# The first mixture's up and down products as separate lists in the order of a fused transformer kernel on one core

## What is computed

```python
# layer 1: two shared experts and eight routed ones, two of them per token; D = 256, H = 128
def _expert(xf, w1, w3, w2):
    return jax.nn.silu(xf @ w1) * (xf @ w3) @ w2
# layer 2: eight experts, hidden width 512
h1 = jnp.einsum('bsd,edf->ebsf', mla_out, w1) + b1[:, None, None, :]
h1 = jax.nn.gelu(h1, approximate=False)
h2 = jnp.einsum('ebsf,efd->ebsd', h1, w2) + b2[:, None, None, :]
moe_out = jnp.einsum('bse,ebsd->bsd', combine, h2)
```

## Time and profile before

| what | value |
|---|---|
| runs | 4680.95, 4694.93, 4677.58 us; median 4680.95 |
| profiled execution | 4675.16 us, of which its span on the core is 4673.4 us |
| TensorE busy | 4280.3 us |
| VectorE busy | 2938.2 us |
| ScalarE busy | 2090.1 us |
| mean granted TensorE clock | 0.957 |

### The profile page before, as it was taken

How to read it: one execution, slowest core, us unless ns; L and a number is a source line. 1 busy time by engine, 2 the same in 40 slices (tenths; PEclk the granted TensorE clock), 3 DMA queues, 4 the chain that set the end, 5 groups by cost and what they waited for, 6 DMA issues and landing times.

```text
span 4673.4 us, 72994 instructions
## 1 busy us (share of the span) xinstructions
PE 4280.3 (92%) x28256; PEld 3232.2 (69%) x28256; DVE 2938.2 (63%) x7633; ACT 2090.1 (45%) x3424; POOL 112.3 (2%) x196
## 2 busy tenths in 40 slices
PE   7898998989989899898998989998899988999889
PEld 4576875758767586575965759667596675966768
DVE  6557676566665666656675566656666566665655
ACT  3543545344553445534355343552435525355242
POOL 0000000000000000000000000000000000000000
PEclk7998999989999899999999999999899999999999
DMA  2010510103101021010310103001030010300012
GB/s 95 1 31 13 199 55 1 43 10 126 47 1 45 25 109 47 2 48 23 118 37 14 39 27 119 28 14 39 28 118 28 14 39 28 118 28 14 30 46 104
DMA packets 51763, 228.00 MB, mean 49 GB/s; under 512 B 4832, under 2 KB 21216, under 8 KB 31584
## 3 DMA queue, kind: packets, MB, share of 16 engines
q1 hardware_dynamic: 51424, 223.33, 13.2%
HBM read 202.34 MB, written 20.97 MB: 48 GB/s over the span
## 4 chain that ended last, share of the span: by engine, by line
PE 78%; DVE 13%; ACT 6%; issue 3%; DMA 0%; DVEq 0%; SPq 0%; ACTq 0%
PE w L540 18%; PE w L550 11%; PE o L674 10%; PE w L795 8%; PE w L785 8%; PE w L607 4%; PE o L667 4%; PE w L524 4%; PE w L590 3%; DVE mx L1187 3%; PE w L533 2%; PE w L642 2%; PE w L686 1%; ACT pt_spread L940 1%; ACT oth L886 1%
## 5 line engine op out<-in xcount | busy, mean ns | idle before, releaser
L1187 DVE TENSOR_REDUCE mx<-w 128x4 f32<-128x1024 f32 x512 | 609.9, 1222 | 203.1 <-PE w L590 174.7
L940 ACT ACTIVATE pt_spread<-w 128x1024 f32<-128x1024 f32 x512 | 518.6, 1023 | 234.1 <-PE w L607 205.1
L674 PE MATMUL o<-pt_spread,va 128*32 128x256 f32 x4096 | 537.1, 406 | 19.7 <-ACT pt_spread L940 19.4
L886 ACT ACTIVATE oth<-w,res 128x256 f32<-128x256 f32 x656 | 277.4, 471 | 567.9 <-PE w L785 460.1
L540 PE MATMUL w<-xnT,stream 128*128 128x256 f32 x1792 | 426.2, 388 | 6.3 <-DVE tmp L1151 3.5
L540 PEld LDWEIGHTS w<-xnT,stream 128*128 128x128 f32 x1792 | 343.1, 194 | 58.3 <-DVE tmp L1151 4.3
L785 PE MATMUL w<-qodd,va_hi 128*128 128x256 f32 x2048 | 349.8, 285 | 1.1 <-DVE x L1157 0.8
L674 PEld LDWEIGHTS o<-pt_spread,va 128*32 128x32 f32 x4096 | 204.9, 113 | 189.2 <-issue 61.3
L590 PE MATMUL w<-ksp,qsp 32*128 32x256 f32 (+1 forms) x2048 | 258.8, 359 | 50.4 <-DVE mx L1187 15.6
L1157 DVE SCALAR_TENSOR_TENSOR x<-w,gate,x 128x256 f32<-128x256 f32 x512 | 223.8, 479 | 121.1 <-PE w L795 96.8
L785 PEld LDWEIGHTS w<-qodd,va_hi 128*128 128x128 f32 x2048 | 285.7, 188 | 10.2 <-issue 2.0
(11 more groups left out here) (255 smaller groups left out, 7735.6 us busy)
## 6 DMA issues: line engine op xcount, KB each, us to landing
stream_lo<-split SPq DMA_DIRECT2D x56, 1024.0 KB, 4.8
va_hi<-split SPq DMA_DIRECT2D x56, 1024.0 KB, 6.9
stream<-in_moe_dram SPq DMA_DIRECT2D x80, 384.0 KB, 3.1
stream<-in_resident_dram SPq DMA_DIRECT2D x8, 2048.0 KB, 7.4
raw<-in_moe_dram SPq DMA_DIRECT2D x8, 1024.0 KB, 6.5
split<-va_hi SPq DMA_DIRECT2D x8, 1024.0 KB, 8.9
split<-stream_lo SPq DMA_DIRECT2D x8, 1024.0 KB, 11.1
stream<-in_resident_dram SPq DMA_DIRECT2D x8, 1024.0 KB, 4.8
```

The costliest lines, as they stand in the source:

```text
L674: mm = pe.matmul(o[g:g + 32, 0:T], by_heads(plan, s)[:, kt, plan.v_of(h), :], p[:, a * 512 + kt * T:a * 512 + (kt + 1) * T], start=(kt == ...
L886: h = act.activation(dst[:, c, :], w[:, c * T:(c + 1) * T], func, bias=bias[:, c:c + 1], **more)
L940: act.activation(exp_buffer(plan.name + ".exp", s, u), w[:, :], ACT.Exp, scale=scale).then_inc(S["s_P"], 1)
L1187: dve.tensor_reduce(mx[s][:, :, 2 * u:2 * u + 2].rearrange("p t a -> p a t"), w[:, :].rearrange("p (a t k) -> p a t k", a=2, t=TT), AX_X, ...
```

## The change

`ASIDE` gets a fourth kind, the steps called `down`, so that the downs of both mixtures form an eleventh list per element: an up may then stand ahead of the down before it in the order. For the first mixture the activations alternate between planes 0 and 1 of `oth` and planes 2 and 3. The waits that the fixed order of up, down, up had made unnecessary are written out: SiLU of expert u waits until VectorE has done the multiplication of expert u - 2; the multiplication of u waits until TensorE has done the down of u - 2; and GELU of the second mixture waits until the down of u - 1 is done. `ORDER` is a new string throughout, over all steps of all layers (slot 1 begins at "B" there, as there are eleven lists). The diff, with all but the first and last line of the two strings left out:

```diff
--- before.py
+++ after.py
@@ -203,8 +203,8 @@
 
 
 
-LISTS = 10
-ASIDE = (("pv", "back"), ("mean", "g1", "g2", "g3", "sum"), ("init",))
+LISTS = 11
+ASIDE = (("pv", "back"), ("mean", "g1", "g2", "g3", "sum"), ("init",), ("down",))
 FIRST = ("l0.ln", "l0.xT", "l0.q", "l0.qs", "l0.max", "l0.peak", "l0.shift")
 
 
@@ -226,46 +226,46 @@
 
 
 ORDER = (
-    "B718B18IB118188IB8HI8888888888I88888B8III88II0I0II550I050I505I0I50I50I5I0550I5050I50I50II505A5AF2A5FAF0AFAFAFAFAFA0FFA0F"
...
-    "GA0AG06A0A0G6A0A0G6A0A06GA0AG060A0607EA0G0A40A0A0A00AAA0A0A0AA0A"
+    "C9K119C11K9CC99K99979999999999I999K9KCKK9910K05K0K50K5K05K0K50K50K50K5K0550K50K50K5050KKK505B5BGB50GB7GBGBGB2GBGBG0BGGBG"
...
+    "0B8J6H0B8JH6B0JHI860B87JH60B8J6H0B8604JH00BF0B0B0B00BBB00BB0BB0B"
 )
 
 
@@ -747,7 +747,7 @@
                     filled(by_features(w, w3, xnT[s], 0, 1, 512))
                 else:
                     pe.wait_ge(*after("s_up1", "f1.up", s, e))
-                    filled(by_tokens(w, oth[s][:, 1:2, :], w2, D, 1))
+                    filled(by_tokens(w, oth[s][:, 2 * (e % 2) + 1:2 * (e % 2) + 2, :], w2, D, 1))
 
             def ffn_2(what, s, e):
                 w = take("f2." + what, s, e)
@@ -1040,7 +1040,9 @@
                     act.activation(gsm[s][:, 4:6], gsm[s][:, 2:4], ACT.Tanh, scale=0.5).then_inc(S["s_act"], 1)
                 elif step == "f1.up":
                     w = full(act, step, s, u)
-                    act.activation(oth[s][:, 0, :], w[:, 0:T], ACT.Silu).then_inc(S["s_silu"], 1)
+                    if u > 1:
+                        act.wait_ge(*after("s_up1", step, s, u - 2))
+                    act.activation(oth[s][:, 2 * (u % 2), :], w[:, 0:T], ACT.Silu).then_inc(S["s_silu"], 1)
 
                 elif step == "f2.split":
                     if u < 2:
@@ -1060,6 +1062,8 @@
                     w = full(act, step, s)
                     evac(kvT[s][0:8, 1, 0:T], w[0:8, 0:T], "s_cTr")
                 elif step == "f2.up":
+                    if u:
+                        full(act, "f2.down", s, u - 1)
                     act.wait_ge(*after("s_uph", step, s, u))
                     w, b = wbank[(UNIT[step, s, u] - 1) % 3], W_["f2_b1"][:, 4 * u:4 * u + 4]
                     biased(oth[s], w, b, 2, ACT.Gelu).then_inc(S["s_gelu2h"], 1)
@@ -1454,7 +1458,9 @@
                 elif step == "f1.up":
                     w = full(dve, step, s, u)
                     dve.wait_ge(*after("s_silu", step, s, u))
-                    dve.tensor_tensor(oth[s][:, 1, :], w[:, 512:512 + T], oth[s][:, 0, :], ALU.mult).then_inc(S["s_up1"], 1)
+                    if u > 1:
+                        full(dve, "f1.down", s, u - 2)
+                    dve.tensor_tensor(oth[s][:, 2 * (u % 2) + 1, :], w[:, 512:512 + T], oth[s][:, 2 * (u % 2), :], ALU.mult).then_inc(S["s_up1"], 1)
                 elif step == "f1.sum":
                     r = u - (MOE1 - MOE1_ROUTED)
                     add_to_x(step, s, u, lambda tt: tg[:, 5:6] if r < 0 else gate[s][:, tt, r:r + 1])
```

More of the change, by code:

```diff
@@ new lines @@
+    "0BGBGBGB0G0B26G6G06DGB060002BB00B0B00HBH0B0HB0BH0DB00B00B0I2BBB0BDB0B00BAB0D0A0BA0BA0500BAB500550A50B5A00BB5B0A0LB50LBLB"
+    "5BBGLB5BG0BLB7L0GBBGBLLB0GGBBGBGG0G3B00BI00388366B0E08B60BBBB86JJHHBBJHBJH860B086J8H600JH860886603BBE0JJH0HB0BJJHH00BE0E"
+    "000B0B0000B00BB0B095050B50B5B0B50B50BB5B55B0B0BBGBGBG7000B00000G00GB0B00G0BG0G0G90BI00B000B55B0BB0BBBB5BB05BB05B0B50B5B5"
+    "BBB457BA0BB0GBG00B0GBGBGBKGB0GGI0G4B1BB1KBB0FBFBAB860JAHB860JHB8AJ6H0B8A6JHB0J8A6HAB0119JH86A099B986990C9986J0HB09C09970"
@@ new lines @@
+    "9JH00CCBK0I190KKBC9B909909BB990990BK0B0K50KB50505050K50K50K5K0550K50K50K50K50K50KB5KKBKBKK5KBB5BGBGBGBG0BG2BGBG0BGB0GG0B"
+    "GBGBGBGB0G6BG6G02G0B6060702BB0B00B00HB0HB0DHB0BH0IBD0000BB20BBBB0DB0B00BAB0D0ABA0005BBA0A0500550BA50B5A00BB5B0LBA05BL0BG"
+    "5B5LB0GBLL0BBBGGBLGBLGBLBGB0B3BGG70G3B00B00E886I63B00EB86BB0BBJ8HJ6HBB0J8H6B0J8H6B0JJH8H686008836E60BB0J0JHH0BBJJ0HHB00E"
+    "000B0B0000B00BB0B0509505B0B50B5B0B50B5B57B5B0B0BB0GBGBG0G000000B00BG00B0GB0G00GIG0B00B00055BBB0B9BBBB05BB05BB0B50B50B5BB"
@@ new lines @@
+    "5B7B45B04B0B0GB0GBG0BGKBGBGBG01G0G1BFB11BBB90B99BB8I96J9H0B989609JHB896JH90B98J69HB90JHB8609JH8690B8690JH7F8610CKB0C0990"
+    "990JIH0CBCK0CB0KKB90900KBKB0B0KB05K0K50505B050K50K50K5K0550K50K50B5K0K50K505KKBKBK5KBB5BGBGBGB0GBGBGBGBGB0GGB0GBGBGB0GB0"
+    "GB6G6G206G0B206002BBB000BI00HB0HB0HBD0BH0D00B7B0B020BBBB0DB0B0B0BAB0DB0A0AA0050BB0550ABA0500BBB550LBA50BLA0B0G5BLB0GLBB5"
+    "LBLBGB5BG0GBLLB0GBBGG70B3G0G0B00B086086386B00EB86BBBB8J6HJHBBJHBJH008608J68H6B0I0JHB886J6H303BBE0JH00BJHJ0HE0EB0000BB000"
@@ new lines @@
+    "00B00BBK0B050505B0B50B5B0B50B5BB557B0B0BB0GB9GBGB0GB0GB0G0B000GG00G0B00B9B00B000BB0IKBB0BB00B5B05B0B5B05B0B50B50B5B5B47B"
+    "4B5BG0BG0G0BB0G0BGBGBG01G0G1BIFBB1BB019F8B96B9B90JHCB989J69H09B98J6H90B98JH6B09J86H0B8J6H90B98690C986J0HB0C970990JHIB0C0"
+    "K01C0BK9KB0K90K09BK0BB0KB0505B05050KB50K50K50K5K0550K505K0K50K50K5K052BKKBK5KBB50BGBGBGBGBGBGBG0BGB0GGBGBG0BGBGB0G6BG6G0"
+    "2G06060B02BB00B0B0H0BH0BD0HB0BH70DB000BB200BIBB0BDB0B00BAB0DB0AA0B5B00A0AB0500550A05B5A00BB5B0AL0B50LBB5LB5BGLBB0GBLBL0G"
@@ L269 @@
+    "B03EB86BBBB0JHJHB86BJHBJ8H6JHB0086B08608J6H0JH8686303BBE0J0H0BJHJ00HEB0E000B00B000B00BB0BB500B5B0B5B0B50BB5050BB55BB5GBG"
+    "B0GBG0BGB70GBGG00G00B00BI0B0000B00B0BB0B00B0B0BB0B050BB5B05B0B50B50B5B50B5B5BG0BGB0G0BGB0GB0GB4GG0G0BBBFBB0BBB8J6H0B8JH6"
+    "0B8J6H0B8JH6B0JHI860B87JH60B8J6H0B8604JH00BF0B0B0B00BBB00BB0BB0B"
 )
```

58 lines of the change are left out of this document (20 added, 38 removed).

## The result

The new kernel takes 4565.92 us (median of four runs, 4561.83 to 4569.61) against 4679.26 us (four runs) before. The ratio is 0.9754 with a 95% interval of 0.9726 to 0.9782: 113 us less, where 45 were forecast. In the new kernel L1457 is L1463, L1151 is L1155, L1206 is L1210, L1187 is L1191, L1043 is L1045, and L1276 is L1280.

The account below looks back on a forecast made before the run. TensorE was taken to bound the kernel, a queue of matrix work with 393 us of holes and 201 us withheld by the clock. Terms of -9.2, -13.8, -8.9, -12 and -1 made -44.9: 4680.95 to 4636 us, range 4618 to 4655.

Parts of the forecast that it names:

- Short waits: First mixture, downs with at most one other down as cover: 36 fall to 12 of 160, -9.2 us.
- waits behind the normalisation: First mixture, down products held up while VectorE normalises the second element's attention output: 29.2 us fall to 15.4, -13.8 us.
- The clock there: First-mixture stretches: with shorter holes TensorE falls to half speed less often, -8.9 us, bounds -11.9 and 0.
- The added waits: New waits on ScalarE and VectorE, each for a step long done: 0, bounded by 6 us.
- the weight loads: Loads into ring slots that later downs free: enough TensorE work stays between, 0, bound +8 us.
- Banks that run out: Rival, first mixture: two ups in a row hold two of three w banks, 4778 us, slower; chance 0.07.
- VectorE's strict order: Rival: the normalisation holds up the multiplication as before, its term and the clock give nothing, 4659 us; chance 0.08.
- more elsewhere: Rival: the whole-order search fills holes in attention as well, 57 us outside the mixture and start, 4591 us; chance 0.20.
- the order elsewhere: Outside the first mixture: the new search covers transpositions of a normalised x better, -12 us, bounds -57 and +23.
- rate of 0.51 us of clock per us of hole: Whole kernel: 201 us withheld by the clock over 393 us of holes, used where nothing better was at hand.
- bound of -57: Best case for the order outside the first mixture: -38 us of holes, with clock at 0.51 each, -57.
- the start: Start of the kernel: the second element's q moves ahead of the first max, -1 us (-3 to +5).

Follow-up runs that it names:

- e8: The new kernel without the 368 added waits: 4568.41 us, ratio 0.9768 to the old kernel.
- e11: Changed code, old order, with 27 first-mixture downs of little cover each swapped with the element's next up: 4693.5 us, ratio 1.0036 to the old kernel.
- e3: Changed code, new order everywhere except in the first-mixture stretches, which follow the old order: 4631.81 us, ratio 0.9909 to the old kernel.
- e4: The new kernel with each first-mixture up that stands ahead of the previous down moved just behind that down: 4754.88 us, ratio 1.0181 to the old kernel.
- e9: Changed code, old order, but new order in the first mixture and what lies around it on both sides: 4658.07 us, ratio 0.9955 to the old kernel.
- e5: Changed code, new order up to the second element's first exponential of layer 0, then old order: 4675.68 us, ratio 1.0008 to the old kernel.
- e1: The changed code with the old kernel's order, step for step: 4682.3 us, ratio 1.0025 to the old kernel.
- e2: Changed code, old order everywhere except in the first mixture, which follows the new order: 4654.26 us, ratio 0.9955 to the old kernel.
- e13: Changed code, new order up to layer 3's values of element 6 (four passes), then old order: 4631.18 us, ratio 0.9914 to the old kernel.
- e14: Changed code, old order up to layer 3's values of element 6, then new order: 4625.93 us, ratio 0.9909 to the old kernel.
- e16: The new kernel with the four matmuls of each of the first element's eight layer 2 maxima done twice: 4563.17 us, ratio 0.9768 to the old kernel.
- e12: The new order with the second element's last first-mixture ups and downs spread among the first element's layer 2 maxima: 4627.27 us, ratio 0.9894 to the old kernel.
- e15: The new kernel with one unneeded matmul ahead of each of the first element's eight layer 2 maxima, 64 in all: 4596.26 us, ratio 0.9832 to the old kernel.
- e10: Changed code with the old order, without the 368 added waits: ratio 1.0008 to the old kernel.
- e6: Changed code, old order, but new order from the first mixture's last sum to the last b2 step in each pass: 4668.57 us, ratio 0.9989 to the old kernel.

## Why the prediction was wrong in size

**Right: the mixture.** Short waits (-9.2) and waits behind the normalisation (-13.8): forecast to leave 3.1 + 15.4 = 18.5 us, measured 9.0 + 7.5 + 1.9 = 18.4, from 41.5. What is late next was named rightly (the bank of the projection), and in the fourth pass its two waits came within 0.02 us. The two terms hold singly too: of the 21 waits for L1463, eight stand behind the normalisation, one in each pass and 0.67 to 0.74 us long (5.7 in sum, with the bank 15.1), and 13 are short ones of 3.3 us together. The holes of the stretches fell by 31 us where these terms say 23, so 8 more went that I had not counted. The clock there was put at -8.9 and gave -11.9, its bound: with no hole over 2 us none of the eight stretches fell below 1.00.

**Right: what costs nothing.** The added waits (e8), the second mixture's overtaking that doesn't occur, and the weight loads in the new order; e11 shows that the last had a bound for a reason, 14.2 us of it. L524's wait for a normalised x was to fall by some 8 and fell by 12.3.

**Right: the rivals left behind.** Banks that run out would show as L540 waiting for L1463; one such wait of 0.4 us is in the list. VectorE's strict order held, but did not decide the time. What came is the rival "more elsewhere" (4591 us, chance 0.20), and beyond it.

**Wrong: the term "the order elsewhere", -12 us.** e3 measures it alone, start included, at -50.5 us against -13 in my sum. One of my signs for being wrong had said so, holes outside the mixture that move by more than 25 us: they moved by 31. Three things were wrong in the step. First, I went by waits that I could name in both orders (28.9 us for a normalised x, the last attention's shifts), and those did move by 12 and +1; the others moved in small pieces all over (holes outside the mixture windows 341 to 310, -31). Several even grew: the maxima's wait L590 for L1191 from 15.6 to 22.4, L674's from 19.4 to 27.2. Second, and larger, the rate of 0.51 us of clock per us of hole. It is a mean over the kernel and says nothing of a change: outside the mixture the holes fell by 31 us and the clock by 47; in e4 the holes rose by 148 against the new kernel and the clock account by 6; in e9 they went opposite ways. Half of those 47, 24 us, lie in the second part of the attention stretches alone; at my rate all of the 12 us less of waiting for a normalised x, wherever they lie, are 6 us of clock. The clock hangs on where the thin stretches lie and what follows them, and for that I should have opened the windows of the eight attention stretches, where 124 of the 201 us lay in plain view, 0.83 to 0.93 in each. I had read windows for the mixture only. Third, my bound of -57 used the same rate, so it took no account of a clock that moves by itself; with the mixture's 32 it would have given 4591, and the measured time is 25 below.

**Too small, as it seems: the start, -1 us.** The clock withheld up to the first mixture is 36 us before and 20 after. It is not steady: over the nine profiled kernels with the old start it is 20 to 37 us, with the new one, nine as well, 15 to 21. e5, against e1, gives 8 us, within overlapping intervals.

**Open.** How e1's 2.5 parts in a thousand come about; what part of the 38 us that e2 and e3 leave over is the seams and what is a real interplay of the two parts; why the medians of e13 and e14 add up to less than their profiled executions. That a shorter mixture gives the attention behind it a better clock was not shown: e9 has the first without the second. What the new freedom is worth to an order made for it is open as well: the best order without it was not searched for.

None of the kernels beats the new one by more than the measurement can tell (e16 4563.17, e8 4568.41, the new kernel 4565.92).

## What to carry to other kernels

When an order is searched anew over everything, the part that the code change touches is the smaller question: read holes and granted clock by stretch over the whole span, and ask first what the new order does in the stretches with the lowest clock. Holes and clock are two accounts with no fixed rate between them. And pieces of a searched order are not to be swapped by hand or moved to another order: of the hand changes here, e11 took 22 us of waits out and gained nothing, e12 cost 61 us and e4 189 against the new kernel. Their lists of waits show why: each moved step also frees a slot or a bank that another step had counted on.

## What the runs showed of the hardware

TensorE fell to 1.2 GHz in stretches without one long hole: in layer 2's maxima, where in the new kernel its waits are 0.2 to 2.1 us and its groups of four matmuls 0.8, and in the attention of the block behind them, where the old kernel's third pass stays at half speed for 27 us with no wait over 1.3 us. Over the whole stretches of 114 to 134 us the clock is 0.83 to 0.93. Doubling the maxima's products brought the product behind them from 3.20 to 1.97 us. The Trainium skill ("TensorE: Matmul & The Clock Gate", section on a second failure mode of the clock gate) reports of a bf16 kernel that goes through its PSUM banks in turn that short idle times between its groups of matmuls come often enough to make the clock go back and forth. In fp32 this trace agrees (the maxima: waits of at most 2.1 us, half speed for 10 to 14 us of each pass). Filling them cost at least as much as it gave here: e15 +30 us, e16 no change.

Instructions in the same order do not always get the same clock. Up to the first mixture, the old order was withheld 20 to 37 us in nine profiled executions (20 in e10, 36 in before, 37 in e6).
